# The first layer norm of two blocks computed with tokens on partitions and turned on TensorE

## What is computed

```python
mod = (silu(c) @ wmod).reshape(1, 6, 1, -1)
sa, ca, ga, sb, cb, gb = (mod[:, i] for i in range(6))   # ga, gb: |.| kept at least 0.25
h = layernorm(x, eps=1e-5) * (1 + ca) + sa
x = x + ga * attn(h)
h = layernorm(x) * (1 + cb) + sb
x = x + gb * ffn(h)

def attn(h):                    # rms(z) = z / sqrt(mean(z*z) + eps)
    q, k, v = split(rms(h) @ w_qkv.T, 3)          # 512 features each
    q, k = rms(q), rms(k)
    w = exp(k)
    y = sigmoid(q) * (cumsum(w * v) / (cumsum(w) + 1e-6))
    u, g = split(y @ w_swiglu.T, 2)               # 2048 each
    return h + u * silu(g) @ w_out.T
# ffn: gate/up and down matmuls with weights decoded from 4 bits, then rms
```

## Time and profile before

| | us |
|---|---|
| median of three runs | 1877.7 (1877.66 to 1877.93) |
| the profiled execution, own time | 1878.42 |
| its span | 1876.6 |
| PE busy | 1842.5 (98%) |
| DVE busy | 1378.4 (73%) |
| ACT busy | 918.7 (49%) |
| POOL busy | 793.3 (42%) |

### The profile page before, as it was taken

One profiled execution on the slowest core, in us unless ns is written; L12 is line 12 of the kernel. 1 busy time (PEld: TensorE's weight loads), 2 busy tenths in 40 slices (PEclk: granted clock), 3 DMA queues, 4 the chain that ended last, 5 costly groups with the idle time before them and its releaser, 6 DMA issues. The chain is left out here.

```text
span 1876.6 us, 24600 instructions
## 1 busy us (share of the span) xinstructions
PE 1842.5 (98%) x8354; PEld 827.9 (44%) x8354; DVE 1378.4 (73%) x1898; ACT 918.7 (49%) x1406; POOL 793.3 (42%) x561
## 2 busy tenths in 40 slices
PE   6999999999999999999999999999999999999997
PEld 2444444444444444444444444444344444444443
DVE  6998677667767875867776786664788777877876
ACT  5864354245235334423533431221676776776774
POOL 2666332232223223322322321221567676667765
PEclk9999999999999999999999999999999999999999
DMA  9423122120311212122020121213311011011011
GB/s 320 135 79 102 56 95 76 42 94 11 101 45 64 68 37 94 29 83 84 25 95 9 50 72 31 91 39 111 129 46 36 33 68 68 1 68 68 1 46 68
DMA packets 78222, 129.90 MB, mean 69 GB/s; under 512 B 7232, under 2 KB 35904, under 8 KB 76480
## 3 DMA queue, kind: packets, MB, share of 16 engines
q1 hardware_dynamic: 78144, 128.91, 20.5%
HBM read 89.54 MB, written 39.35 MB: 69 GB/s over the span
## 5 line engine op out<-in xcount | busy, mean ns | idle before, releaser
L780 PE MATMUL bank<-Y,wsw 128*128 128x512 f16 x3072 | 683.1, 379 | 1.6 <-ACT V L932 1.0
L780 PEld LDWEIGHTS bank<-Y,wsw 128*128 128x128 f16 x3072 | 299.7, 98 | 368.0 <-ACT V L932 3.3
L1210 POOL TENSOR_TENSOR late<-late 128x512 f16<-128x512 f32 x128 | 174.6, 1364 | 669.2 <-ACT late L1016 668.5
L757 PE MATMUL bank<-late,wout 128*128 128x512 f16 x1536 | 352.4, 379 | 0.4 <-POOL late L1210 0.4
L2214 DVE SCALAR_TENSOR_TENSOR f_A<-bank,gu_s,f_A 128x512 f32<-128x512 f32 x352 | 260.8, 741 | 122.4 <-ACT f_A L2025 117.0
L2101 POOL TENSOR_TENSOR f_A<-f_A 128x512 f32<-128x512 f32 x175 | 274.6, 1569 | 169.5 <-DVE f_A L2214 168.0
L2025 ACT ACTIVATE f_A<-bank,gu_s 128x512 f32<-128x512 f32 x328 | 225.4, 688 | 149.2 <-PE bank L1955 147.9
L1917 PE MATMUL bank<-f_HH,f_down_hi 128*128 128x512 f16 x704 | 265.8, 379 | 2.1 <-DMA f_down_lo<-down_lo_scratch 0.7
L1277 DVE TENSOR_TENSOR late<-late,bank 128x512 f32<-128x512 f32 x128 | 87.5, 683 | 231.7 <-PE bank L780 230.6
L1008 ACT ACTIVATE late<-bank 128x512 f32<-128x512 f32 x128 | 76.4, 597 | 339.6 <-PE bank L780 324.7
L757 PEld LDWEIGHTS bank<-late,wout 128*128 128x128 f16 x1536 | 150.2, 98 | 184.8 <-issue 5.9
(11 more groups left out here) (232 smaller groups left out, 1984.1 us busy)
## 6 DMA issues: line engine op xcount, KB each, us to landing
X<-xT SPq DMA_DIRECT2D x14, 1024.0 KB, 5.3
room<-packed SPq DMA_DIRECT2D x48, 176.0 KB, 2.4
h_scratch<-X SPq DMA_DIRECT2D x8, 1024.0 KB, 4.2
f_X<-x_scratch SPq DMA_DIRECT2D x8, 1024.0 KB, 5.4
x_scratch<-X SPq DMA_DIRECT2D x28, 256.0 KB, 2.2
h_scratch<-SQ SPq DMA_DIRECT2D x28, 256.0 KB, 3.5
outT<-f_X SPq DMA_DIRECT2D x7, 1024.0 KB, 4.2
room<-wswT SPq DMA_DIRECT2D x4, 1024.0 KB, 6.9
```

Of the source, the lines that this page charges most:

```text
L757: mm = nc.tensor.matmul(O_BANK[c][:], wout[:, pw, j, c * P:(c + 1) * P], UG[:, j % 2, px, :], start=(j == 0 and pw == 0 and px == 0), stop ...
L780: mm = nc.tensor.matmul(out[:], wsw[:, pw, k, col:col + P], Y[:, px, k, :], start=(k == 0 and pw == 0 and px == 0), stop=(k == DT - 1 and ...
L1210: nc.gpsimd.tensor_tensor(UG[:, j % 2, 1, :], G, UG[:, j % 2, 0, :], ALU.subtract).then_inc(UG_low, 1)
```

## The change

For blocks 0 and 1, x is loaded with tokens on partitions, as four tiles of 128 tokens by 512 features (`x_early`, 256 KB each; block 1's tiles go to RD, `late` and two tiles of X2). DVE takes BN_STATS of each and BN_AGGR (`early_stats`), ACT the root of 128x4 (`ln_root`), DVE the reciprocal of 128x4 and one TENSOR_SCALAR per tile, minus mean times inverse deviation (`early_norm`). PE turns the tiles back to features on partitions, 16 transposes of 128x128 fp32 per block against an identity (`turn`): block 0's ahead of the first group, block 1's in two halves, after groups 4 and 6. `early_h` reads the turned tile from its bank, times 1+ca plus sa, which is h; `early_high` is then a copy to f16 and `early_low` a subtraction. `early_modulate`, `early_centre`, `early_scale`, `early_add_x` and `reduce_tiles` go, with the MEAN sums and the early VAR sums. Block 0's HSQ sum is now three adds on POOL, between its low parts of PK and PQ, and one matmul after group 3; it goes to bank 2, which block 1's turn (banks 3 and 5) does not use, and waits for `h_ready`. The first 2 MB of wmod are loaded as two halves with PK between them. POOL and DVE make the identity at the start. ACT's PQ split comes behind the first two K copies, PV's ahead of block 0's h squares.

```diff
+    x_early = x.rearrange("(b i p) d -> p b i d", b=NB, p=P)
...
+        ident = sb("ident", [P, P], F32)
...
-        R_BANK = {MEAN: bank[2], VAR: bank[2], HSQ: bank[2], QSQ: bank[3], KSQ: bank[0]}
+        R_BANK = {VAR: bank[2], HSQ: bank[2], QSQ: bank[3], KSQ: bank[0]}
...
+        EARLY_XT = [XT, [RD[:, :], late[:, 0:T], X2[:, 2, :], X2[:, 3, :]]]
+        TURN_BANK = [bank[2:6], [bank[3], bank[5], bank[3], bank[5]]]
...
-        EARLY_BANK = {(MEAN, 0): bank[2], (VAR, 0): bank[2], (HSQ, 0): bank[2],
-                      (MEAN, 1): O_BANK[1], (VAR, 1): O_BANK[1], (HSQ, 1): O_BANK[1],
-                      (KSQ, 0): O_BANK[0], (KSQ, 1): R_BANK[QSQ]}
-        EARLY_DEV = {(VAR, 0): bank[2][:], (VAR, 1): O_BANK[1][:], (KSQ, 0): O_BANK[0][:], (QSQ, 0): R_BANK[QSQ][:],
+        EARLY_BANK = {(HSQ, 0): bank[2], (HSQ, 1): O_BANK[1], (KSQ, 0): O_BANK[0], (KSQ, 1): R_BANK[QSQ]}
...
+            def load_wmod_first(half):
+                cols = slice(half * DT, half * DT + DT)
+                sp.dma_start(wmod_first.rearrange("p (n k) -> p n k", k=DT * P)[:, cols, :], v["wmodT"][:, cols, :]
+                             ).then_inc((wmod_loaded[0], wmod_rest)[half], 16)
+            for i in range(4):
+                sp.dma_start(XT[i], x_early[:, 0, i, :]).then_inc(x0_loaded[max(i - 1, 0)], 16)
             sp.dma_start(c_silu_row, v["c_row"].to_broadcast([P, DT * P])).then_inc(c_ready, 16)
-            load_wmod(0)
+            load_wmod_first(0)
             load_piece(PK)
-            sp.dma_start(X2[:], xT_t[:, :, tok(1)]).then_inc(x1_loaded, 16)
+            load_wmod_first(1)
+            for i in range(4):
+                sp.dma_start(EARLY_XT[1][i], x_early[:, 1, i, :]).then_inc(xt_loaded, 16)
             load_piece(PV)
...
             def bank_read(kind, b):
-                if kind == VAR:
-                    pe.wait_ge(centred, DT * (b + 1))
+                if kind == HSQ and early(b):
+                    pe.wait_ge(h_ready, DT * (b + 1))
...
-            def reduce_tiles(kind, b):
-                for c in range(DT):
-                    if kind == MEAN:
-                        tile, sums = X01[b][:, c, :], tile_sum
-                        pe.wait_ge(x1_loaded, 16)
-                    else:
-                        tile, sums = RING[c], sq_sum[0]
-                        pe.wait_ge(squared[0], DT * nth_squares(kind, b) + c + 1)
-                    if c == 0:
-                        bank_read(kind, b)
-                    mm = nc.tensor.matmul(sum_bank(kind, b)[:], ones[:], tile, start=c == 0, stop=c == DT - 1)
-                    if c in (1, 2):
-                        mm.then_inc(sums, c)
-                mm.then_inc(reduced[0], 1)
+            def turn(b, tiles):
+                pe.wait_ge(centred, DT * (b + 1))
+                for c in tiles:
+                    if b:
+                        pe.wait_ge(h_ready, DT + max(c - 1, 0))
+                    for i in range(4):
+                        mm = nc.tensor.transpose(TURN_BANK[b][c][:, i * P:(i + 1) * P], EARLY_XT[b][i][:, c * P:(c + 1) * P], ident[:])
+                    mm.then_inc(turned, 1)
...
-                    if b == 0 and n in (0, 3):
-                        reduce_tiles({0: VAR, 3: HSQ}[n], n == 0)
-                    if b == 0 and n in (5, 9):
-                        reduce(*{5: (KSQ, 0), 9: (HSQ, 1)}[n])
+                    if b == 0 and n in (4, 6):
+                        turn(1, range(n - 4, n - 2))
+                    if b == 0 and n in (3, 5, 9):
+                        reduce(*{3: (HSQ, 0), 5: (KSQ, 0), 9: (HSQ, 1)}[n])
...
-            pe.wait_ge(const_ready, 1)
-            reduce(MEAN, 0)
-            reduce_tiles(VAR, 0)
-            reduce_tiles(MEAN, 1)
+            pe.wait_ge(mod_step, 6)
+            turn(0, range(DT))
...
-            def early_modulate(b, c):
-                act.wait_ge(H_low, DT * b + c + 1)
-                nc.scalar.activation(X01[b][:, c, :], X01[b][:, c, :], ACT.Identity,
-                                     bias=mod[:, SA][:, c:c + 1]).then_inc(h_ready, 1)
             def early_high(b, c):
-                act.wait_ge(scaled, DT * b + c + 1)
-                if c == 0 and b == 0:
-                    act.wait_ge(mod_summed, first_cols)
-                elif c == 0:
+                act.wait_ge(h_ready, DT * b + c + 1)
+                if c == 0 and b:
                     act.wait_ge(h_stored, 16)
                     act.wait_ge(squared[0], DT * (nth_squares(HSQ, 0) + 1))
-                nc.scalar.activation(H01[b][:, 0, c, :], X01[b][:, c, :], ACT.Identity,
-                                     bias=mod[:, SA][:, c:c + 1]).then_inc(H_high, 1)
+                nc.scalar.activation(H01[b][:, 0, c, :], X01[b][:, c, :], ACT.Copy).then_inc(H_high, 1)
...
+            ln_root(0)
             split(PK)
             act.wait_ge(mod_summed, first_cols)
             nc.scalar.activation(mod[:, CA], mod[:, CA], ACT.Identity, bias=1.0).then_inc(c_ready, 1)
-            sqrt(VAR, 0)
             for c in range(DT):
                 early_high(0, c)
             split(PV)
-            early_square(VAR, 1)
-            for c in range(DT):
-                early_modulate(0, c)
-            sqrt(VAR, 1)
-            split(PQ)
+            early_square(HSQ, 0)
+            ln_root(1)
             for c in (0, 1):
                 copy_out(0, c)
                 early_square_qk(KSQ, 0, K, c)
-            early_square(HSQ, 0)
-            for c in range(DT):
-                early_high(1, c)
-            for c in (2, 3):
-                copy_out(0, c)
-                early_square_qk(KSQ, 0, K, c)
+            split(PQ)
+            copy_out(0, 2)
+            early_square_qk(KSQ, 0, K, 2)
             sqrt(HSQ, 0)
-            for c in range(DT):
-                early_modulate(1, c)
-            early_square(HSQ, 1, (0, 1))
+            copy_out(0, 3)
+            early_square_qk(KSQ, 0, K, 3)
+            early_high(1, 0)
+            early_high(1, 1)
             sqrt(KSQ, 0)
-            early_square(HSQ, 1, (2, 3))
+            early_high(1, 2)
+            early_high(1, 3)
+            early_square(HSQ, 1)
...
+            nc.gpsimd.iota(ident[:].bitcast(I32), pattern=[[1, P]], base=0, channel_multiplier=-1).then_inc(shift_ready, 1)
             nc.gpsimd.iota(lane[:], pattern=[[0, 1]], base=0, channel_multiplier=1).then_inc(shift_ready, 1)
             split_low(PK)
+            early_add_squares(HSQ, 0)
             split_low(PQ)
...
+            def early_stats(b):
+                for i in range(4):
+                    if b:
+                        dve.wait_ge(xt_loaded, 64)
+                    else:
+                        dve.wait_ge(x0_loaded[max(i - 1, 0)], 2 * 16 if i < 2 else 16)
+                    nc.vector.bn_stats(parts[:, i, :], EARLY_XT[b][i]).then_inc(tile_sum, 1)
+                dve.wait_ge(tile_sum, 8 * b + 4)
+                if b:
+                    dve.wait_ge(centred, DT)
+                for i in range(4):
+                    nc.vector.bn_aggr(stats[:, :, i], parts[:, i, :]).then_inc(tile_sum, 1)
+            def early_norm(b):
+                ln_inverse(b)
+                dve.wait_ge(recip[VAR], b + 1)
+                for i in range(4):
+                    nc.vector.tensor_scalar(EARLY_XT[b][i], EARLY_XT[b][i], stats[:, 0, i:i + 1], stats[:, 1, i:i + 1],
+                                            ALU.subtract, ALU.mult).then_inc(centred, 1)
+            def early_h(b, c):
+                dve.wait_ge(turned, DT * b + c + 1)
+                if b and c >= 2:
+                    dve.wait_ge(turned, 2 * DT)
+                nc.vector.tensor_scalar(X01[b][:, c, :], TURN_BANK[b][c][:], mod[:, CA][:, c:c + 1], mod[:, SA][:, c:c + 1],
+                                        ALU.mult, ALU.add).then_inc(h_ready, 1)
+            def early_low(b, c):
+                dve.wait_ge(H_high, DT * b + c + 1)
+                nc.vector.tensor_tensor(H01[b][:, 1, c, :], X01[b][:, c, :], H01[b][:, 0, c, :], ALU.subtract).then_inc(H_low, 1)
...
+                    if part == 0 and i == DT:
+                        dve.wait_ge(wmod_rest, 16)
...
+            nc.vector.tensor_scalar(ident[:], ident[:].bitcast(I32), 0, None, ALU.is_equal).then_inc(shift_ready, 1)
...
-            early_add_x()
-            early_centre(0)
+                clamp(mod[:, GA], 7)
+                clamp(mod[:, GB], 11)
+            early_stats(0)
+            early_norm(0)
             modulation(0)
-            inverse(VAR, 0)
             dve.wait_ge(c_ready, 16 + 3)
-            early_scale(0)
-            early_low(0, (0, 1))
-            early_centre(1, (0,))
-            early_low(0, (2,))
-            early_centre(1, (1,))
-            early_low(0, (3,))
-            early_centre(1, (2, 3))
+            early_h(0, 0)
+            early_h(0, 1)
+            early_low(0, 0)
+            early_h(0, 2)
+            early_low(0, 1)
+            early_h(0, 3)
+            early_low(0, 2)
```

(74 more changed lines are left out.)

45 lines of the change are left out of this document (17 added, 28 removed).

## The result

| | before | changed |
|---|---|---|
| median, us | 1877.66 (1876.02 to 1879.02, 15 runs) | 1881.09 (1879.57 to 1882.13, 14 runs) |
| ratio | | 1.0018, 95% interval 1.0011 to 1.0025 |
| profiled execution, own time | 1878.42 | 1880.59 |
| its span | 1876.6 | 1878.8 |
| first SwiGLU matmul | 105.19 | 107.99 |

A fifteenth run of the changed kernel took 1951.79, with a mean granted clock of 0.946 for 0.993 to 0.996 in the others, and is left out, as is one of 4755.32 of the kernel before, run beside e5 to e8. The kernel is 3.4 us slower: inside the 0.2% of "no change", but the interval does not hold 1. The forecast was +1.7, in the range, so the sign was right and the size half.

A forecast was written before the change was run, and what follows sets the result against it. PE, busy 98% of the span, was taken as the bound. Start -5.5, PE work -3.4 and waits +10.5 gave +1.6, as the chain's 1.7, so 1879.4 us; range 1873.0 to 1884.0.

The forecast's parts named there:

- The start of block 0: Shorter norm beside the modulation, then `early_h` and `early_low`: PE's first group starts at 22.4, 5.5 us before 27.89.
- The transpose: PE's price for one 128x128 fp32 transpose: taken as 0.2 us, so sixteen per block take 3.2.
- D: Rival, slower by more: transposes cost 0.4 each, both fp32 load passes paid; 6.9 late, 1884.6; chance 0.18.
- C: Rival with a dearer transpose, its text cut here; its time lay inside 1873.9 to 1881.5; chance 0.08.
- POOL and DVE: DVE operations with SBUF inputs are held beside POOL's: block 1's norm takes 8.5 us, `V<-K,V` ends at 67.0, 2.6 later.
- B: Rival: POOL holds only two-input DVE operations, block 1's norm runs free; 1.3 early, 1876.4; chance 0.12.
- PE's waits: PE waits 1.7 at block 1's turn, 2.1 for HSQ1's sum, 3.1 for QSQ's, 4.3 before the 82.44 group.
- -5.5, -3.4 and +10.5: Terms up to the 82.44 group: earlier start, less PE work, and added PE waits; together +1.6.
- Behind it all is as now ... Nothing behind gives it back: Behind `V<-K,V` little changes: the 82.44 group comes at 84.2, 1.7 late, and that loss stays.
- carried to the end one for one: What the first SwiGLU matmul, at 105.19 before, gains or loses reaches the end in full.
- A: Rival, the lead is kept: DVE and POOL fall kindly, 6.7 early or 5.0 with a late clock; 1871.0 to 1872.7; chance 0.17.

The follow-up runs named there:

- e5: Changed kernel with POOL's split of PU0 behind the adds of Q's squares and POOL waiting for `K<-Q,K` before PO0's split: 1878.94 against 1877.68, 1.0006.
- e8: Changed kernel with wmod's two halves loaded one behind the other, ahead of PK: 1882.49 against 1877.68 for the kernel before, 1.0023.
- e1: Changed kernel with block 0's HSQ sum back on PE as four fp32 matmuls, without POOL's adds: 1878.48 against 1877.77 for the kernel before, 1.0003.
- e2: Changed kernel with POOL's split of PU0 moved behind its adds of Q's squares: 1880.68 against 1877.77 for the kernel before, 1.0015.
- e6: Changed kernel with POOL's split of PQ moved behind its adds of K's squares: 1878.87 against 1877.68 for the kernel before, 1.0005.
- e10: e5 and e6 together, plus 13 unused f16 matmuls in PE's wait ahead of the first SwiGLU matmul: 1874.96 against 1877.28 for the kernel before, 0.9986.
- e4: Changed kernel with 18 unused f16 matmuls in PE's wait ahead of the group at 83.72: 1879.13 against 1877.77 for the kernel before, 1.0007.

## Why the prediction was right, and where it was off

**The start of block 0**: 22.4 forecast, 21.62 measured, because the loads landed 1.2 us earlier. Counted from `c_row` the gain is 5.1, not the 5.5 of the forecast. The steps were as told: root at 11.6, behind ACT's table load, norm done at 14.1, modulation bound by DVE without a gap. One row was mis-sized: `early_h` with two pointers out of a bank takes 0.72 from start to start (two in 1.53), not 0.61.

**The transpose**: 0.2 taken. Behind each other they are 0.213 apart ahead of the first group and 0.109 apart in block 1: eight cost 0.9, not 1.6. D falls: each of the 32 has one weight load. C, the rival with the chance of 0.08, had reckoned with a dearer one than even the 0.213; no run shows that term, and that C's time comes near the measured 1881.09 is a coincidence. Whether a row of them brings the clock up is open. In the changed kernel the sixteen, 3.4 us of them, are all at the lower level, but in e1 the last three are 0.11 apart, and in the changed kernel so low are also the ordinary matmuls of the group at 21.62, 0.43 apart for their first 3.9 us, behind a wait of 3.76. (The column of the granted clock reads 1.00 there, so this goes by spacing.)

**POOL and DVE**: 8.5 forecast for the norm, 8.3 measured; end of `V<-K,V` 67.0 and 66.64 (with the loads where they were before, 67.9). Each of the four operations of the norm ends 0.28 or 0.29 behind the POOL operation that held it; 0.2 was forecast. The TENSOR_SCALAR with two pointers, of which the trace of before has none beside POOL, is held too: beside POOL 1.29 and more, in e1 0.54. B falls with it. The row of L1478 carried the estimate. That two SBUF inputs don't run beside POOL, for which the earlier trace rows show one meeting, holds in the whole trace of before: 51 such operations ended 0.28 to 0.55 behind POOL's, and 21 had POOL wait for them (the counts are in the last section).

**PE's waits**, ahead of the turn, for the HSQ1 sum, for QSQ's and ahead of the group of 82.44: 1.7, 2.1, 3.1 and 4.3 forecast, 1.37, 3.49, 1.22 and 4.24 measured. The sum is near, the two in the middle had their sizes exchanged. The group of 82.44: 84.2 forecast, 83.72 measured. Of the sum's terms up to there, -5.5, -3.4 and +10.5, the traces have -6.3, -2.4 and +9.9. PE's term has two errors that partly cancel: the transposes cost 1.8, not 3.2, and a half-speed stretch of 1.7 at 59.74 was not in it. The 83.72 has luck in it: counted from `c_row` the group is 2.3 to 2.5 late, not 1.7.

**What failed** is the step "Behind it all is as now ... Nothing behind gives it back". Nothing ahead of the SwiGLU stage gave it back, but behind that wait it was not as now: a wait of 4.24 us costs its length and then 1.7 us more of half-speed matmuls. The rows had shown it after the wait of 3.85, and I used it for the first group only. With that term the forecast would have been 1.7 + 1.7 = 3.4. That this is the difference of the medians is in part luck: between the two profiles the terms are 1.3 and 1.7, 2.8 at the SwiGLU stage, and 0.6 was given back near the end. So "carried to the end one for one" failed by that 0.6 too. A is refuted by the waits; the place of the loss was right, its size was half.

**What I would not have seen**: which meeting counts. e1 removes the norm's 6.4 us and gains 0.4 on the chain, because PE's sum is then the bound; e2 removes 4.6 and runs into the next split; e5 clears that too, and the last chain then meets POOL. e5 and e6 together bring PE's group to 77.15, 5.3 before that of the kernel before, and e10 adds the filled wait; the last chain is still the bound there.

## What to carry to other kernels

When an operation moves earlier on DVE, list all long POOL operations that it will now stand beside (an operation of 0.5 to 0.7 took 4.2 to 4.6 beside a split), not only the one beside it now, and the ones that those behind it will meet. Where PE is the bound, price its waits by length plus the half-speed stretch behind them (none to 2.5 us behind waits of 2.37 to 4.24 in these runs); a few unused matmuls in a wait that can't be removed are cheap, and e4 and e10 gained 2.0 and 1.6 by them. A lead at the start is worth only what the slowest chain behind it can take over.
